# Quad 9 of the scan goes to GpSimd, its one-element products go, and one transfer adds both logarithms

## The reference

```
dt = softplus(dt @ W_dt)                      # 512 channels
A_disc = exp(A * dt)                          # decay of each state
Bx = dt * B * xs                              # input of each state
h  = A_disc * h + Bx                          # scan over the tokens
y  = sum over n of h * C                      # 512 channels
out = (y * silu(res)) @ W_out
x = x + layernorm(residual + out)
```

## Time and profile before

| | us |
|---|---|
| median of 3 runs | 2177.78 (2175.21 to 2179.42) |
| the profiled execution's own time | 2176.57 |
| its span | 2174.8 |
| first scan to last | 93.7 to 1950.4 |
| DVE busy | 1880.0 (86%) |
| GpSimd busy | 1810.6 (83%) |
| PE, ACT busy | 1681.9 (77%), 1412.7 (65%) |

### The profile page before, as it was taken

One profiled execution on the slowest core, in us unless ns is written; L12 is line 12 of the kernel. 1 busy time (PEld: TensorE's weight loads), 2 busy tenths in 40 slices (PEclk: granted clock), 3 DMA queues, 4 the chain that ended last, 5 costly groups with the idle time before them and its releaser, 6 DMA issues. The chain is left out here.

```text
span 2174.8 us, 23216 instructions
## 1 busy us (share of the span) xinstructions
PE 1681.9 (77%) x5620; PEld 649.5 (30%) x5620; DVE 1880.0 (86%) x2071; ACT 1412.7 (65%) x2547; POOL 1810.6 (83%) x768
## 2 busy tenths in 40 slices
PE   7777879888788979787878797888888785552690
PEld 3222323232232323232323232323223231211690
DVE  2477999999999999999999999999999999998221
ACT  2565676867686767777777777676768676542121
POOL 0275999999998989898999999999999898960456
PEclk9897988889897979797979898988989796656795
DMA  2663367576667574757566666756676758318742
GB/s 92 165 178 89 87 137 157 127 159 143 146 147 155 118 173 105 170 115 156 128 145 138 143 157 132 159 128 151 146 151 141 151 115 178 80 56 277 246 103 63
DMA packets 168837, 304.63 MB, mean 140 GB/s; under 512 B 27632, under 2 KB 87794, under 8 KB 168720
## 3 DMA queue, kind: packets, MB, share of 16 engines
q1 hardware_dynamic: 137696, 240.13, 44.7%
q0 software_dynamic: 30640, 62.32, 16.1%
q10 hardware_dynamic: 384, 1.05, 0.2%
HBM read 77.82 MB, written 39.52 MB: 54 GB/s over the span
## 5 line engine op out<-in xcount | busy, mean ns | idle before, releaser
L1041 DVE TENSOR_TENSOR_SCAN room<-pa,carry,room 128x512 f32<-128x512 f32 x1024 | 1243.3, 1262 | 72.6 <-ACT pa L887 59.4
L1240 POOL TENSOR_TENSOR room<-room 128x2048 f32<-128x2048 f32 x256 | 1172.8, 4590 | 145.3 <-ACT carry L880 145.2
L887 ACT ACTIVATE pa<-room,neg_a 128x512 f32<-128x512 f32 x1024 | 695.1, 687 | 355.2 <-DVE room L1041 343.9
L536 PE MATMUL py<-room,blk 128*32 128x512 f32 x2048 | 337.5, 732 | 148.9 <-DVE gate L1047 94.3
L1027 DVE TENSOR_TENSOR room<-room,pb 128x2048 f32<-128x2048 f32 x192 | 433.7, 2259 | 0.3 <-DMA room<-du 0.3
L1233 POOL TENSOR_TENSOR room<-room,b_rep 128x2048 f32<-128x2048 f32 x64 | 290.3, 4536 | 6.3 <-DVE room L1041 5.3
L600 PE MATMUL pp<-xs,w_dtx 128*128 128x512 f32 x512 | 255.7, 635 | 18.0 <-DVE du L967 11.7
L609 PE MATMUL pb<-bc,sel_b 32*128 32x512 f32 x288 | 202.3, 789 | 69.7 <-DVE room L1027 69.7
L564 PE MATMUL pp<-xsp,w_conv 128*128 128x512 f32 x512 | 244.7, 612 | 7.9 <-ACT xsp L754 7.9
L556 PE MATMUL pp<-xnt,w_in 128*128 128x512 f32 x256 | 168.3, 792 | 69.9 <-ACT xs L761 57.0
L600 PEld LDWEIGHTS pp<-xs,w_dtx 128*128 128x128 f32 x512 | 97.2, 200 | 171.4 <-issue 145.1
(11 more groups left out here) (189 smaller groups left out, 1867.5 us busy)
## 6 DMA issues: line engine op xcount, KB each, us to landing
room<-du SPq DMA_DIRECT2D x1016, 128.0 KB, 2.4
du<-du POOLq DMA_DIRECT2D x56, 512.0 KB, 6.7
room<-in_L_ffn_w_dram SPq DMA_DIRECT2D x39, 512.0 KB, 7.5
room<-bc_scratch SPq DMA_DIRECT2D x64, 256.0 KB, 5.1
du<-late POOLq DMA_DIRECT2D x28, 512.0 KB, 6.3
combine_scratch<-zeros SPq DMA_DIRECT2D x16, 520.0 KB, 10.0
xt<-in_L_attn_x_dram SPq DMA_DIRECT2D x16, 512.0 KB, 4.3
b_rep<-bc_scratch SPq DMA_DIRECT2D x64, 128.0 KB, 5.4
```

The source lines that it names most:

```text
L536: mm = pe.matmul(py[32 * j:32 * j + 32, :], blk[:], h[:, quad % 4, j, :], start=(g == 0), stop=(g == 3), tile_position=(0, 32 * j))
L887: act.activation(pa[:, decay_bank(t), :], rep[:, c % 2, t % 4, 0, :], ACT.Exp, scale=neg_a[:, a_column(t):a_column(t) + 1]).then_inc(s_exp, 1)
L1041: v.tensor_tensor_scan(h[:, quad % 4, t % 4, :], pa[:, decay_bank(t), :], bq[:, quad % 2, t % 4, :], carry[:, par, t:t + 1], ALU.mult, ALU ...
L1240: pool.tensor_tensor(h[:, quad % 4], h[:, quad % 4], c_rep[:, par, quad % 4, :].unsqueeze(1).broadcast_to((P, 4, T)), ALU.mult).then_inc(s ...
```

## The change

Quad 9 goes from VectorE to GpSimd. The seven one-element products go; the transfers carry the waits themselves, with one more on a semaphore that has long been set, and registers for the waited values are computed ahead (`settled`). Both additions of the logarithm are one transfer of 1 MB with a semaphore of its own (`d_ln`); block 0's u waits for it, where before it waited for the first half alone. `SPREADS` has seven entries where it had nine, since B's group for quads 1, 5 and 9 is now needed on VectorE only at quad 13.

```diff
-VECTOR_QUADS = (0, 2, 4, 6, 8, 9, 10, 11, 12, 13, 14, 15)
-POOL_QUADS = (1, 3, 5, 7)
+VECTOR_QUADS = (0, 2, 4, 6, 8, 10, 11, 12, 13, 14, 15)
+POOL_QUADS = (1, 3, 5, 7, 9)
...
-SPREADS = ((0, 0, 0, 14), (2, 1, 2, 15), (1, 1, 9, 6), (2, 0, 10, 8), (3, 1, 11, 9), (0, 0, 12, 10), (1, 1, 13, 11),
-           (2, 0, 14, 12), (3, 1, 15, 13))
+SPREADS = ((0, 0, 0, 15), (2, 1, 2, 14), (3, 0, 11, 8), (0, 1, 12, 10), (1, 0, 13, 11), (2, 1, 14, 12), (3, 0, 15, 13))
...
-    return 16 * (3 * (i - 2) + n)
+    return 16 * (2 * (i - 2) + n)
...
                         if second:
-                            act.wait_ge(d_sum[0], added(j + 2, 3))
-                            act.wait_ge(d_sum[1], added(j + 2, 2))
+                            act.wait_ge(d_ln, 16 * (j + 1))
...
+                        if t == at_slots["add_ln"]:
+                            settled(logarithms(i, 0), added(i, 2), added(i, 1))
+                            pool.wait_ge(s_const, 3)
+                            pool.wait_ge(s_ln, logarithms(i, 0))
+                            pool.wait_ge(d_sum[0], added(i, 2))
+                            pool.wait_ge(d_sum[1], added(i, 1))
+                            pool.dma_start(du[:, :, 0, :], logs[:], accum_op=ALU.add).then_inc(d_ln, 16)
...
                             if t == at_slots["add_e"][pair]:
+                                settled(DC * i + 2 * pair + 2, NU * i + use("dt", 2 * pair + 1) + 1)
+                                pool.wait_ge(s_const, 3)
                                 pool.wait_ge(s_sp, DC * i + 2 * pair + 2)
                                 pool.wait_ge(s_free, NU * i + use("dt", 2 * pair + 1) + 1)
-                                pool.tensor_tensor(pad3[:, pair:pair + 1], mhalf[:, 0:1], mhalf[:, 0:1], ALU.mult)
                                 pool.dma_start(du[:, both, 0, :], du[:, both, 1, :], accum_op=ALU.add).then_inc(d_sum[pair], 16)
...
-                                pool.wait_ge(d_sum[c // 2], added(i, 3))
+                                pool.wait_ge(d_ln, 16 * (i - 1))
+                                if c >= 2:
+                                    pool.wait_ge(d_sum[1], added(i, 2))
...
-                        pool.tensor_tensor(pad3[:, 6:7], mhalf[:, 0:1], mhalf[:, 0:1], ALU.mult)
                         pool.dma_start(z[:], xo[:], accum_op=ALU.add).then_inc(s_x1, 16)
```

More of the change, by code:

```diff
@@ L50 @@
     keep_in=(-9, -3, 3, 9), act_xs=(-7, -1, 5, 11), silu_x=13,
-    pe_bc=(18, 19), act_bc=21, store_bc=22, load_c=23, load_b=60, sel=(58, 62, 87, 95, 99, 103, 107, 111, 115),
+    pe_bc=(18, 19), act_bc=21, store_bc=22, load_c=23, load_b=60, sel=(58, 62, 99, 103, 107, 111, 115),
     pe_dt=((14, 15), (23, 24), (30, 31), (37, 38)), abs=(16, 26, 33, 40), exp=(17, 27, 34, 41),
     pe_res=(27, 30, 33, 36), act_res=(29, 32, 35, 38), silu_g=84, keep_r=24,
-    ln=44, rest=((36, 37), (52, 53)), add_e=(30, 42), add_rest=(38, 54), add_ln=(44, 44), u=(48, 48, 60, 61),
+    ln=44, rest=((36, 37), (52, 53)), add_e=(30, 42), add_rest=(38, 54), add_ln=44, u=(48, 48, 60, 61),
     rep=(50, 63, 79, 95))
@@ L62 @@
     pe_dt=((15, 16), (23, 24), (30, 31), (37, 38)), abs=(17, 25, 32, 65), exp=(18, 26, 33, 65), o1=(18, 27, 34, 66),
-    pe_bc=(19, 20), act_bc=21, store_bc=25, load_c=26, load_b=27, sel=(28, 29, 87, 95, 99, 103, 107, 111, 115),
+    pe_bc=(19, 20), act_bc=21, store_bc=25, load_c=26, load_b=27, sel=(28, 29, 99, 103, 107, 111, 115),
     ln=((19, 0, 1), (27, 1, 2), (77, 2, DC)), s=(20, 28, 79, 82), o2=(21, 29, 80, 83), o3=(22, 30, 81, 84),
@@ L71 @@
     pe_dt=((29, 30), (35, 36), (39, 40), (42, 43)), abs=(31, 38, 41, 45), exp=(32, 39, 42, 45), o1=(33, 40, 43, 46),
-    pe_bc=(33, 34), act_bc=35, store_bc=36, load_c=37, load_b=60, sel=(58, 62, 87, 95, 99, 103, 107, 111, 115),
+    pe_bc=(33, 34), act_bc=35, store_bc=36, load_c=37, load_b=60, sel=(58, 62, 99, 103, 107, 111, 115),
     ln=((36, 0, 1), (48, 1, DC)), s=(38, 50, 53, 56), o2=(39, 51, 54, 57), o3=(40, 52, 55, 58),
@@ L289, in scan_layers @@
         pad2 = sb("pad2", [P, 1], U32)
-        pad3 = sb("pad3", [P, 7])
         mv2 = sb("mv2", [P, SUB, 2])
@@ L329, in scan_layers @@
         d_sum = [sem("first_pair_added"), sem("second_pair_added")]
+        d_ln = sem("logarithms_added")
         d_rep = [sem(f"rep_loaded_{c}") for c in range(DC)]
@@ L1177, in head, with settled @@
                         pool.tensor_tensor(nm[:], mean[:], rs[:, SUB:], ALU.mult).then_inc(s_nm, 1)
+                def settled(*values):
+                    for value in values:
+                        if not isinstance(value, int):
+                            pool.compute_val(value)
                 def prep(t, i, par):
@@ L1184, in prep @@
                             if t == at_slots["add_e"][pair]:
+                                settled(DC * i + 2 * pair + 2, NU * i + use("dt", 2 * pair + 1) + 1)
+                                pool.wait_ge(s_const, 3)
                                 pool.wait_ge(s_sp, DC * i + 2 * pair + 2)
                                 pool.wait_ge(s_free, NU * i + use("dt", 2 * pair + 1) + 1)
-                                pool.tensor_tensor(pad3[:, pair:pair + 1], mhalf[:, 0:1], mhalf[:, 0:1], ALU.mult)
                                 pool.dma_start(du[:, both, 0, :], du[:, both, 1, :], accum_op=ALU.add).then_inc(d_sum[pair], 16)
[L1189 to L1193, removed]
                             if t == at_slots["add_rest"][pair]:
+                                settled(DC * i + 2 * pair + 2, added(i, 1), 16 * (i - 1))
+                                pool.wait_ge(s_const, 3)
                                 pool.wait_ge(s_s, DC * i + 2 * pair + 2)
-                                pool.wait_ge(d_sum[pair], added(i, 1 + pair))
-                                pool.tensor_tensor(pad3[:, 4 + pair:5 + pair], mhalf[:, 0:1], mhalf[:, 0:1], ALU.mult)
+                                pool.wait_ge(d_sum[pair], added(i, 1))
+                                if pair == 1:
+                                    pool.wait_ge(d_ln, 16 * (i - 1))
                                 pool.dma_start(du[:, both, 0, :], du[:, both, 1, :], accum_op=ALU.add).then_inc(d_sum[pair], 16)
@@ L1219, in post @@
                     if t == POST["x1"] and not final(j):
+                        settled(j + 1, 16 * (j + 1))
+                        pool.wait_ge(s_const, 3)
                         pool.wait_ge(s_z2, j + 1)
                         pool.wait_ge(d_xo, 16 * (j + 1))
-                        pool.tensor_tensor(pad3[:, 6:7], mhalf[:, 0:1], mhalf[:, 0:1], ALU.mult)
                         pool.dma_start(z[:], xo[:], accum_op=ALU.add).then_inc(s_x1, 16)
```

## The result

The changed kernel took 2191.14 us (median of 5, 2189.81 to 2196.04), the kernel before 2179.42 in the same comparison; the ratio is 1.0065 (95% interval 1.0052 to 1.0078). So the change is slower, by about 12 us in the medians (14 by the ratio): inside the predicted range of 2167 to 2196, outside the likeliest case's own 2178 to 2183, and not the "same" that the forecast named.

What follows compares the result with a forecast made beforehand. Two loops within one or two us of each other bound the kernel, through VectorE's second half and through dt; the latter would bind after. Profiled 2176.6 + 2 (+0.15 times 13 tiles) + 1.2 = 2180 us, range 2167 to 2196.

Steps and rivals of the forecast that it cites:

- the likeliest case: Whole kernel: forecast 2180 us, own range 2178 to 2183; "same" had chance 0.40.
- Loop B: Loop through VectorE's second half, quads 9 to 14, and back to GpSimd: 114.68 us per tile, to become 113.78.
- in3: Start of quad 3's inputs on GpSimd, the zero point of each tile's times: 1283.36 in tile 10, 1398.04 in tile 11.
- Loop C: Loop through dt: logarithm, block 0's u, SP's copies, next tile's quads 0 and 1; 114.48 into odd, 115.35 into even tiles.
- mostly gone: Sign of being right: GpSimd's idle time before the states, 145 us in all, would mostly vanish.
- the 1.43: Merged transfer's generation time in us; anything over it was named a sign that the forecast is wrong.
- the rival that counted pieces: Merged transfer's issue costs by its pieces, generation 2.48 for 1.24: 2196 us; both slower rivals together chance 0.30.
- The one with an early landing: Merged transfer lands in 5.6 us or less, so the loop through VectorE's second half binds: 2168 us, chance 0.25.
- no bound: GpSimd's own instruction list, summed to 113.4 us per tile, was judged not to limit the kernel.
- the middle between two ends: Change per tile taken as +0.15 us, between -0.06 and +0.38; times 13 tiles, +2.
- The two slower rivals: Merged transfer's issue costing by its pieces, or second add_e landing too late: 2196 us each, together chance 0.30.
- the cover of add_e gone: Second add_e lands in 7 us instead of 5.6, logarithm's issue 1.3 later: 2196 us; both slower rivals together chance 0.30.

Runs made afterwards that it cites:

- a_early_ln: Changed kernel with the logarithm in two transfers, the first issued one states product earlier, u at slot 46 for 48: 2162.43 us, 0.9931 of the kernel before.
- a_two_ln: Changed kernel with the logarithm added in two transfers again, block 0's u waiting for the first alone: 2173.94 us, 0.9978 of the kernel before.
- a_load_b: Changed kernel with B's four copies for GpSimd issued at slot 49, ahead of block 0's copies, instead of slot 60: 2185.29 us, 1.0034 of the kernel before.
- b_q9_pool: Kernel before with only quad 9's inputs moved to GpSimd; one-element products and two transfers stay: 2188.18 us, ratio 1.0040.
- b_early_ln: Kernel before with the logarithm's first half at slot 43, u at 46, no one-element products, quad 9 on VectorE: 2174.62 us, ratio 0.9982.

## Why the prediction was right and wrong

**Right: which loop takes over.** Loop B fell as worked out: quad 9 is scanned 47.6 after in3 (predicted 47.6), with 1.5 of wait (1.3), and its period in a_early_ln, where it binds alone, is 113.77 in two tiles and 113.90 in the mean (113.78). Loop C binds, by the wait at VectorE's quad 0. GpSimd's idle time before the states fell from 145.3 to 60.1, which is more than half and not "mostly gone". GpSimd works 110.81 per tile for the "about 112": that figure left out the issue that merging saves (a_two_ln, with two transfers, has 111.83).

**Right: loop C's first half.** Logarithm's issue 70.57 in tile 10, 70.63 over twelve tiles (predicted 70.83). Landing 8.57 and 8.14 behind it in tiles 10 and 11 (8.33 and 8.0). u at 79.20 and 78.74 (79.16 and 78.83), idle before it 2.57 (2.4). The landing over the whole run (us to landing, minimum, median, maximum):

```profile
L1192 POOL DMA_DIRECT2D du<-late x14: 1282/1454/1490, 315.1 to 1824.9; - x14
...
DMA to landing us min/median/max: 8.0/8.2/8.7
```

Its generation took 1.28 to 1.49. The median, 1.45, lies just past the 1.43 that the prediction named as a sign against itself; but that is 0.2 more than 1.24 and not twice it, so the rival that counted pieces fell. The one with an early landing fell too (8.0 at the least). The Trainium skill's fit (DMA: Bandwidth & Descriptors, Anatomy of one DMA) gives an estimate of 4.4 for 1 MB; the runs disagree, with 5.0 for 512 KB issued by itself (a_early_ln) and 8.0 for 1 MB.

**Wrong: the tile's start.** The sum took the stretch from VectorE's quad 0 to the end of quad 1 from the kernel before, as if it were fixed work: 17.88 into an odd tile, and 19.16, which runs on to in3, into an even one. In tiles 10 and 11 of the changed kernel the same stretches measured 18.54 and 20.52 (20.44 to the end of quad 1); over the twelve tiles the stretch to the end of quad 1 grew by 1.1. That is 0.66 + 1.36 = 2.02 of the 2.1 by which the two tiles (115.60 + 116.35 = 231.95, in3 to in3) exceed the predicted 229.83.

The rest is two small terms of opposite sign. In3 of tile 11 came 0.44 behind the scan instead of 0.08, since GpSimd was still at its list, late by the 1.77 that it had waited for B's copies; the prediction put that list at 113.4 and "no bound". And VectorE's quad 0 came 0.3 sooner behind u and the landing than the sum had it.

The stretch is not fixed work. Two things lengthen it.

Into odd tiles TensorE is the link. ScalarE's xs, for which it waits, comes later once VectorE has stood at the landing, so TensorE stands still 3.81 ahead of the next tile's first projection, where it stood 1.89. The first four products then run at a lower granted clock: 0.59 of 2.4 GHz in the mean of that stretch for 0.72, which is more of it at the lower of the two levels, 1.2 GHz. They take 3.21 for 2.66 and hand their result to ScalarE, which starts to copy it 9.29 behind the start of VectorE's quad 0 (before: 8.71) and makes the decays that VectorE awaits behind that copy. The four products after the change, and before:

```profile
1395.77 3.21 PE L555 MATMUL pp<-xnt,w_in 128*128 128x512 f32 x4 [3.81 <-ACT xs L760]
```

```profile
1384.98 2.66 PE L556 MATMUL pp<-xnt,w_in 128*128 128x512 f32 x4 [1.89 <-ACT xs L761]
```

The clock in these stretches (behind the busy times: granted clock, DMA share, GB/s), after and before:

```profile
1395.80:1399.00 3.20, 3.20 (x6) 1.31 (x7) 3.20 (x3) 1.21 (x3) 3.20 (x1) 0.59 1.02 213
```

```profile
1385.00:1387.60 2.60, 2.60 (x5) 1.05 (x6) 2.60 (x3) 1.22 (x3) 2.60 (x1) 0.72 1.02 214
```

The difference, 0.55, is that of VectorE's wait, 2.18 for 1.63. The wait in the kernel before:

```profile
1389.93 2.46 DVE L1041 TENSOR_TENSOR_SCAN room<-pa,carry,room 128x512 f32<-128x512 f32 x2 [1.63 <-ACT pa L887]
```

Over the six odd tiles the means say the same: the four products take 3.69 at a granted clock of 0.52, before 2.83 at 0.73, and the wait is 2.65 for 1.71, nearly all of the 0.97 by which the odd tiles' start grew. In a_two_ln, where VectorE hardly waits for block 0 (0.04), TensorE stands still 1.99 for the changed kernel's 3.79, the products take 2.62, and the wait is 1.56. That the clock is the cause is read from these rows; no run changed the clock alone.

Into even tiles the branch is the link. ScalarE's first decay behind it stood idle 4.16, of which the profile can name no releaser; at the same place before it was 2.83, and in a_early_ln, where block 0 has landed long before, 1.60. VectorE's two waits grew from 0.77 and 1.66 to 1.57 and 2.19. After, before, and a_early_ln:

```profile
1514.68 0.69 ACT L885 ACTIVATE pa<-room,neg_a 128x512 f32<-128x512 f32 x1 [4.16 <-issue]
```

```profile
1502.06 0.69 ACT L887 ACTIVATE pa<-room,neg_a 128x512 f32<-128x512 f32 x1 [2.83 <-DVE room L1041]
```

```profile
1486.73 0.69 ACT L886 ACTIVATE pa<-room,neg_a 128x512 f32<-128x512 f32 x1 [1.60 <-DVE room L1040]
```

The copies of B that a_load_b moved account for 0.8 of the 1.15 by which even tiles' start grew. The Trainium skill (Runtime: NRT & Kernel Launch, Instruction fetch mechanics) says that a taken branch outside the pages that an engine holds must fetch its target by DMA first; the trace agrees. It shows a queue that it calls instruction, whose packets of 8 KB move around each branch; here from 1504.8 to 1515 in the changed kernel (packets, MB, share of the 16 engines):

```profile
q14 instruction: 4, 0.03, 1.4%
```

The first of these packets starts to move 2.91 behind VectorE's branch in the mean of five, before 1.44, and in a_early_ln 0.75, where VectorE and ScalarE take only 3.04 and 3.00 from the branch to the next instruction. Over the thirteen profiles, the later that packet starts, the longer VectorE's branch takes, nearly without exception. Which packet belongs to which engine isn't recorded. Standing still is not the reason here: in a_two_ln VectorE waits 0.27 for block 0 in these tiles, and yet they start in 20.3, with 4.85 and 4.97 behind the branch. What makes up the other 0.35 stays open.

**Wrong: the middle between two ends.** The prediction had -0.06 and +0.38 per tile and took +0.15, arguing that tiles 10 and 11 were quicker than the mean. That was a way of hoping that the slow tiles would become like them. All twelve tiles bind on loop C now, and pay for their starts: +1.37 per tile. The upper end was the better value, and above it a term for the start was missing, of 1.1 per tile or 14 us.

**The rivals that came nearest in size, not in mechanism.** The two slower rivals gave 2196; their mechanisms (a doubled generation, the cover of add_e gone) are not what happened: the generation is told above, and the second add_e had landed at least 0.56 before the logarithm's issue in every tile. That the range took in 2191 is owed to them, and so to luck.

**The one-element products.** The prediction priced seven at 0.9 per tile by the spacing of starts. b_q9_pool and a_two_ln differ by them alone, and GpSimd's busy time per tile is 112.94 and 111.83: 1.1 for seven, near the 0.9 and far from the 2.9 of the recorded spans.

## What to carry to other kernels

When two loops run within a microsecond of each other, price the second one before relieving the first, and ask what hands work on to it: here one instruction less to issue made the first consumer wait for twice the data. A stretch that follows a wait is not fixed work: here TensorE's granted clock was lower after it had stood still, and a branch that fell among transfers took longer, so what came next was longer than it had been measured. Two loops that lie so close have to be relieved together: quad 9's move without its products gained 0.22% (a_two_ln), the earlier link of loop C 0.18% (b_early_ln), and both 0.69% (a_early_ln).

## What the runs showed of the hardware

On GpSimd the recorded start of an instruction can lie ahead of its work. In b_q9_pool the list has no gap ahead of u, and the records behind each transfer grow (GpSimd in time, tile 10):

```profile
1347.36 0.18 POOL L1196 TENSOR_TENSOR pad<-mhalf 128x1 f32<-128x1 f32 x1
...
1352.79 0.65 POOL L1186 TENSOR_TENSOR pad<-mhalf 128x1 f32<-128x1 f32 x1
...
1358.21 1.12 POOL L1191 TENSOR_TENSOR pad<-mhalf 128x1 f32<-128x1 f32 x1
...
1359.12 1.62 POOL L1191 TENSOR_TENSOR pad<-mhalf 128x1 f32<-128x1 f32 x1
...
1364.54 4.35 POOL L1205 TENSOR_TENSOR du<-du,xs 128x512 f32<-128x512 f32 x2
```

```profile
1367.69 12.47 SPq L437 DMA_DIRECT2D room<-du  x16
```

A product of one element records 0.18, then 0.65, 1.12 and 1.62: each transfer leaves some 0.48 us of lag, and the lag goes when GpSimd waits. u's record starts 6.2 behind the logarithm's issue, which looks earlier than before (7.6), but SP's copies start 3.15 behind it, where it was 1.28 before: the work was late all the same. So in a gapless stretch with transfers even the spacing of starts misleads, and the time is read from ends, or from who is released. The Trainium skill (Perfetto Trace Analysis, GPSIMD Engine Instruction) calls these spans unreliable and advises the spacing; the spans bear that out, and the spacing fails here too.
